# A StyleGAN-like convolution chain: one 7-tap convolution per sample in place of a blurred upsampling and a downsampling, and another order of the stages

## The chip, the cores and the metric

The kernel runs on one core of a Trainium2 chip. The metric is the device time of one execution in microseconds (us). The core has TensorE (PE, matmul; PEld is its weight load), VectorE (DVE), ScalarE (ACT), GpSimd (POOL) and SyncE (SP, here only DMA issue).

## The reference, cut to what matters

x has 128 samples of 32 channels by 512 positions. Four layers are applied; each is a conditioned chain of four small 1D convolutions (`_layer`), and a linear layer over the 512 positions (512 by 512) with a residual.

```
s = style @ mw.T + mb                     # 64 style numbers per sample -> 32
weight = SCALE * w * s[:, None, :, None]  # so every sample has its own 3-tap weights
weight = weight * rsqrt(sum(weight**2) + EPS)
'same':       conv(x, weight) + b
'upsample':   conv_transpose(x, weight, stride 2) + b, then blur with 2*[1,3,3,1]/8
'same':       conv(x, weight) + b
'downsample': blur with [1,3,3,1]/8, conv(stride 2) + b
y = x after the four convolutions
x = x + linear(y)   # layer 1: top-2 of 8 LoRA experts; layer 2: a LoRA chosen by sample group;
                    # layer 3: top-1 of 4 LoRA experts; layer 0: LoRAs folded into the weight
```

Upsampling, blurring, the third convolution, blurring and downsampling are linear, so they can be composed into fewer convolutions with longer kernels, apart from the few positions at each end.

## The kernel before, in words

Sixteen samples form a group: 4 row blocks of 32 channels fill the 128 partitions, times 4 columns. There are 8 groups and 4 layers, so 32 phases; phase n is one group in one layer, and two groups alternate, since phase n needs the result of phase n - 2. Eight phases make a step: two of layer 0, two of layer 1 and so on. The work of a loop turn n on PE is the convolutions of phase n and the linear layer of phase m = n - 1. Layers 0 and 2 are called plain below, layers 1 and 3 have an adapter.

Small tiles: the convolutions are matmuls of 32 by 32 (or 64 by 32, 32 by 64) weights, sixteen (or eight) of which stand side by side in the array. One step is one tap for all 16 samples. All convolution operands are fp32, and each matmul instruction has two records in the trace.

PE's order in a turn, written out by hand in the block at the end of `main_program`:

- `conv0(n)` (L1003): first convolution, 3 steps of 512 columns, 48 matmuls.
- `turn(m)` (L1078): 16 transposes of y3 into four PSUM banks; ACT copies them rounded (`y3t_hi`), DVE subtracts (`y3t_lo`).
- `conv2(n, 0)`, `conv2(n, 1)` (L1052): upsampling, blur and third convolution composed to per-sample kernels `wv`; 3 paired taps of 64 output columns, two single taps, and 16 one-column matmuls for the ends ("ghosts"), each.
- `adapter(m)` (L1095) in layers 1 and 3: 24 or 12 matmuls of 512 columns. It waits for all of `y3t_lo`.
- `base(m, b)` (L1137): 12 matmuls of 128 by 128 by 512 for each of four blocks of tokens b. In phases m % 8 = 1 and 4 `effective` (L1108) also makes the weights of the chosen LoRA, which DVE adds to a raw weight (`w_sum`, L957).
- `products(n + 1)` (L1027): products of the second and third convolutions' weights for the next phase, 5 steps (3 of 96 columns, 2 of 32). POOL then sums neighbours in three passes (`blurred`, L698).
- `down(n, 0)`, `down(n, 1)` (L1068): blur and downsampling, 3 taps, 48 matmuls of 64 by 32.

ACT and DVE evacuate each half of the banks (`evacuate_0`, `evacuate_2`, `evacuate_3`), POOL scales the input (`xs`, L716), adds the bias (L729) and makes the low halves of weights (`w_lo`, L723). Two sets of four PSUM banks exist, `bank_a` and `bank_b`, with fixed roles. Semaphores order everything; no scheduler reorders.

A first program (`setup_program`) computes styles, demodulation, end corrections (`bias_q`, L453) and weights, once; the main program starts when it is over.

## Time and profile before

| | |
|---|---|
| median of 3 runs | 1303.74 us (1299.21 to 1305.76) |
| profiled execution, its own time | 1306.01 us |
| its span | 1304.2 us |
| PE busy | 1233.0 us (95%) |
| DVE / ACT / POOL busy | 496.3 / 356.1 / 546.2 us |
| mean granted clock of TensorE | 0.987 |

PE records overlap, as matmuls are pipelined: the length of a stage is best read as the difference of two starts. The time of a group of small matmuls is the union of its records, not the mean of one times the count.

### The profile page before, as it was taken

The page shows a single profiled execution, that of the slowest core. Times are in us where ns is not written, and L with a number is a line of the kernel's source. Part 1 is how long each engine was busy: PE and PEld are TensorE (multiplying, and loading weights), DVE is VectorE, ACT ScalarE, POOL GpSimd, SP SyncE. Part 2 cuts the span into 40 slices and gives each one's busy share as a digit, 9 for nine tenths or more (in the row PEclk, how much of TensorE's full clock was granted, in tenths as well). Part 3 has the DMA queues.
Part 4 walks back from the last instruction along what each step waited for, and adds up shares of the span by engine and source line. Part 5 has one row for each costly group of instructions (what it writes and reads, how often), then busy time and mean ns, then how long its engine had stood idle before and what let it go on. Part 6 is the DMA issues. An engine that isn't in the chain of part 4 may idle for free.

```text
span 1304.2 us, 45847 instructions
## 1 busy us (share of the span) xinstructions
PE 1233.0 (95%) x21400; PEld 704.6 (54%) x21400; DVE 496.3 (38%) x975; ACT 356.1 (27%) x757; POOL 546.2 (42%) x417
## 2 busy tenths in 40 slices
PE   5847999999999999999999999999999999999997
PEld 5323556555555555565565555565565554665555
DVE  5612324344333333434333333434333434433343
ACT  2213313223322222313223222312323222312321
POOL 3156641444443442644323543644413544634400
PEclk9968999999999999999999999999999999999999
DMA  8232300002221200000301300000211200000101
GB/s 285 114 105 101 115 17 2 2 3 59 98 105 62 99 3 2 3 2 25 134 27 42 131 3 2 2 2 13 103 53 58 99 3 2 2 2 3 67 2 65
DMA packets 20828, 65.66 MB, mean 50 GB/s; under 512 B 4032, under 2 KB 4416, under 8 KB 16160
## 3 DMA queue, kind: packets, MB, share of 16 engines
q1 hardware_dynamic: 18960, 60.85, 12.8%
q8 instruction: 168, 2.75, 0.9%
q10 hardware_dynamic: 1680, 1.89, 0.5%
q14 instruction: 20, 0.16, 0.0%
HBM read 43.85 MB, written 18.87 MB: 48 GB/s over the span
## 4 chain that ended last, share of the span: by engine, by line
PE 87%; DVE 4%; POOL 1%; issue 1%; ACT 0%; DMA 0%; DVEq 0%; POOLq 0%
PE bank_b L1137 26%; PE bank_a L1068 13%; PE bank_a L1052 11%; PE bank_b L1052 11%; PE bank_b L1003 8%; PE bank_b L1095 5%; PE bank_a L1078 5%; PE bank_a L1027 3%; PE bank_b L1149 2%; PE bank_b L1118 1%; DVE w_sum L957 1%; PE bank_b L1130 1%; POOL xs L716 1%; POOL sum_v L698 1%; DVE z L939 1%
## 5 line engine op out<-in xcount | busy, mean ns | idle before, releaser
L698 POOL TENSOR_TENSOR sum_v<-raw_v 128x768 f32<-128x768 f32 x32 | 58.9, 1842 | 626.5 <-ACT raw_v L760 626.5
L1137 PE MATMUL bank_b<-w_hi,y3t_hi 128*128 128x512 f32 x512 | 210.0, 410 | 12.4 <-DVE w_sum L957 12.1
L1137 PE MATMUL bank_b<-w_hi,y3t_lo 128*128 128x512 f32 x512 | 203.0, 396 | 2.2 <-issue 2.2
L1137 PE MATMUL bank_b<-w_lo,y3t_hi 128*128 128x512 f32 x512 | 202.4, 395 | 0.1
L1068 PE MATMUL bank_a<-y,w_down 64*32 64x512 f32 x3072 | 173.6, 594 | 1.5 <-ACT wv L762 1.5
L1052 PE MATMUL bank_a<-y,wv 32*64 32x512 f32 (+2 forms) x3584 | 145.8, 480 | 2.3 <-issue 2.3
L1052 PE MATMUL bank_b<-y,wv 32*64 32x512 f32 (+2 forms) x3584 | 142.3, 480 | 1.8 <-ACT y L741 1.8
L895 DVE TENSOR_TENSOR x<-bank_b,x 128x512 f32<-128x512 f32 x96 | 66.4, 692 | 202.2 <-PE bank_b L1137 166.0
L753 ACT ACTIVATE y<-bank_a,cb,tab 128x512 f32<-128x512 f32 x64 | 49.7, 776 | 319.4 <-PE bank_a L1068 319.4
L1003 PE MATMUL bank_b<-xs,cw 32*32 32x512 f32 x3072 | 112.0, 615 | 15.3 <-POOL xs L716 15.3
L1137 PEld LDWEIGHTS bank_b<-w_hi,y3t_hi 128*128 128x128 f32 x512 | 96.8, 189 | 50.9 <-DVE w_sum L957 15.6
L1137 PEld LDWEIGHTS bank_b<-w_hi,y3t_lo 128*128 128x128 f32 x512 | 96.6, 189 | 25.9 <-issue 3.1
L1068 PEld LDWEIGHTS bank_a<-y,w_down 64*32 64x32 f32 x3072 | 55.3, 106 | 102.2 <-issue 102.2
L1137 PEld LDWEIGHTS bank_b<-w_lo,y3t_hi 128*128 128x128 f32 x512 | 97.0, 189 | 20.3 <-issue 0.6
L716 POOL TENSOR_TENSOR xs<-x,tab 128x512 f32<-128x512 f32 x96 | 97.3, 1043 | 8.9 <-DVE x L895 8.9
L1052 PEld LDWEIGHTS bank_a<-y,wv 32*32 32x32 f32 (+1 forms) x3584 | 45.0, 114 | 100.9 <-issue 100.4
L875 DVE TENSOR_SCALAR y<-bank_a,tab,cb 128x512 f32<-128x512 f32 x64 | 51.8, 810 | 121.4 <-PE bank_a L1068 121.4
L1003 PEld LDWEIGHTS bank_b<-xs,cw 32*32 32x32 f32 x3072 | 48.0, 104 | 76.5 <-issue 48.1
L854 DVE TENSOR_SCALAR y<-bank_b,tab 128x512 f32<-128x512 f32 x64 | 48.9, 807 | 100.8 <-PE bank_b L1003 100.8
L1052 PEld LDWEIGHTS bank_b<-y,wv 32*32 32x32 f32 (+1 forms) x3584 | 44.7, 114 | 76.4 <-issue 73.3
L881 DVE TENSOR_TENSOR y3t_lo<-bank_a,y3t_hi 128x512 fp32r<-128x512 f32 x128 | 79.5, 684 | 15.0 <-ACT y3t_hi L768 15.0
L861 DVE TENSOR_SCALAR y<-bank_a,tab 128x512 f32<-128x512 f32 x64 | 48.9, 806 | 90.4 <-PE bank_a L1052 90.4
(172 smaller groups left out, 1553.0 us busy)
## 6 DMA issues: line engine op xcount, KB each, us to landing
w_hi<-w_scratch SPq DMA_DIRECT2D x9, 1024.0 KB, 5.8
w_lo<-w_scratch SPq DMA_DIRECT2D x9, 1024.0 KB, 8.0
x_in<-in_x SPq DMA_DIRECT2D x32, 256.0 KB, 4.1
out_x<-out_tile SPq DMA_DIRECT2D x32, 256.0 KB, 2.4
w_raw<-w_scratch SPq DMA_DIRECT2D x3, 1024.0 KB, 9.8
w_scratch<-w_hi SPq DMA_DIRECT2D x3, 1024.0 KB, 3.9
w_scratch<-w_lo SPq DMA_DIRECT2D x3, 1024.0 KB, 6.9
w<-in_w SPq DMA_DIRECT2D x2, 1024.0 KB, 13.5
```

Of the source, the lines that this page charges most:

```text
L698: ins = g_.tensor_tensor(dst[:, :, at:at + count].rearrange("p r k o -> p r (k o)"), src[:, :, 0:count].rearrange("p r k o -> p r (k o)"), ...
L716: nc.gpsimd.tensor_tensor(xs[:, b, 1:LEN + 1], src[:, b], column(n, T_S, b).broadcast_to((P, LEN)), ALU.mult).then_inc(xs_ready, 1)
L753: a.activation(y3[:, r], bank_a[r][:], ACT.Identity, bias=keep["cb3"][:, layer(n):layer(n) + 1], scale=column(n, T_A + 3, r)).then_inc(y3_ ...
L875: v.tensor_scalar(y3[:, r], bank_a[r][:], column(n, T_A + 3, r), keep["cb3"][:, layer(n):layer(n) + 1], ALU.mult, ALU.add).then_inc(y3_dve, 1)
L881: v.tensor_tensor(y3t[1][:, k], bank_a[k][:], y3t[0][:, k].bitcast(F32), ALU.subtract).then_inc(y3t_ready, 1)
L895: v.tensor_tensor(result, lin_ps[b][:], x[g][:, b], ALU.add).then_inc(x_ready, 1)
L1003: ins = pe.matmul(banks[r][CH * c:CH * (c + 1)], weights[rows, l, block_], src[rows, (r + c) % ROWS, 1 + shift:1 + shift + LEN], start=(i ...
L1052: ins = pe.matmul(banks[r][to:to + CH * count, at:at + length], wv[rows, a, tap:tap + count].rearrange("p t o -> p (t o)"), y0[rows, a, st ...
L1068: ins = pe.matmul(bank_a[2 * u + h][CH * a:CH * (a + 1)], keep["down"][rows, layer(n), t], y2[u][rows, c, t:t + LEN], start=(t == 0), stop ...
L1078: ins = pe.transpose(bank_a[k][:, P * b:P * (b + 1)], y3[:, b, P * k:P * (k + 1)], ident[:])
L1095: ins = pe.matmul(ps[0:rows], a_l[ai][:, k, col:col + rows], y3t[yi][:, k], start=(k == 0 and i == 0), stop=(k == KB - 1 and i == 2))
L1137: ins = pe.matmul(lin_ps[b][:], y3t[yi][:, k, P * b:P * (b + 1)], w[use(m) % 2][wi][:, k], start=(k == 0 and i == 0), stop=(k == KB - 1 an ...
```

## The change

`conv2` and `down` are replaced by one convolution with seven taps at the sample's own resolution, `conv(n)`: 7 steps of 16 matmuls of 512 columns, and between them 6 steps of 16 one-column matmuls (`END_STEPS`) that correct the first and last positions. Its kernels `wv` come from two rounds of products on PE: `products_raw(n + 1)` (3 steps of 128, 96 and 128 columns; up times same) and `products_all(n)` (7 steps of 288, 224, 224, 192, 192, 96 and 96 columns; times a blurred down kernel from the setup). ACT and DVE evacuate them into `wr` and `wv`; POOL's `blurred` is gone. `evacuate_2` is gone too.

PE's turn is now `products_raw(n + 1)`, `products_all(n)`, `conv0(n)`, `turn(m)`, `linear_front(m)` (adapter, two of the four blocks, `effective`), `conv(n)`, `linear_back(m)`. The bank sets change roles each phase (`banks_x`, `banks_y`). In block 0 of `base` the matmuls with `y3t_hi` come before those with `y3t_lo`, each with its own wait. `turn` and `products_all` have new waits.

In the setup the end corrections take a second round of products through PE (`bias_3`), between the LoRA weights of layer 0 and the effective weights of layer 2, with DVE's down kernels before it; and the matmuls of layer 0's weights wait for `bias_2_ready` in place of `bias_copied`.

PE at the passage from a plain phase's linear layer to the next turn, where `wv` are the sample's kernels, `w_down` the down kernels and `w_hi`, `w_lo` the linear weights. Before:

```order
L1137 MATMUL bank_b<-w_hi,y3t_lo 128x512
L1068 MATMUL bank_a<-y_0,w_down 32x512 x24
L1068 MATMUL bank_a<-y_1,w_down 32x512 x24
L1003 MATMUL bank_b<-xs,cw 32x512 x48
L1078 MATMUL bank_a<-ident,y 128x128 x16
L1052 MATMUL bank_b<-y,wv 64x512 x8
L1052 MATMUL bank_b<-y,wv 32x1 x16
L1052 MATMUL bank_b<-y,wv 64x512 x16
L1052 MATMUL bank_b<-y,wv 32x512 x16
```

And now, to the same point:

```order
L1194 MATMUL bank_b<-w_hi,y3t_lo 128x512 x4
L1076 MATMUL bank_a<-w_up,w2s 32x128 x16
L1076 MATMUL bank_a<-w_up,w2s 32x96 x16
L1076 MATMUL bank_a<-w_up,w2s 32x128 x16
L1092 MATMUL bank_b<-w_down,wr 32x288 x16
L1092 MATMUL bank_b<-w_down,wr 32x224 x32
L1092 MATMUL bank_b<-w_down,wr 32x192 x32
L1092 MATMUL bank_b<-w_down,wr 32x96 x32
L1061 MATMUL bank_a<-xs,cw 32x512 x48
L1130 MATMUL bank_b<-ident,y 128x128 x16
L1189 MATMUL bank_a<-w_hi,y3t_hi 128x512
```

The products stand ahead of conv0, the down convolution is gone, and the linear layer follows the transposes at once; conv2 stood between them before.

PE in an adapter phase of layer 1, from the transposes on, now:

```order
L1061 MATMUL bank_b<-xs,cw 32x512 x48
L1130 MATMUL bank_a<-ident,y 128x128 x16
L1144 MATMUL bank_b<-y3t_hi,a_hi 128x512
L1144 MATMUL bank_b<-y3t_lo,a_hi 128x512
L1144 MATMUL bank_b<-y3t_hi,a_lo 128x512
```

The adapter's matmuls, which want `y3t_lo` whole, moved from behind conv2 to right behind the transposes.

PE in the setup, from the end corrections (`bias`) to the effective weights (`gmat`), before:

```order
L453 MATMUL w_ps<-bias_v,bias_q 128x64 x12
L463 MATMUL w_ps<-b,a 128x512 x8
L470 MATMUL mod_ps<-bs_raw,as_raw 128x512 x2
L470 MATMUL mod_v_ps<-bs_raw,as_raw 128x512
L470 MATMUL var_ps<-bs_raw,as_raw 128x512
L480 MATMUL w_ps<-b,gmat 128x512 x8
```

Now, where the rows for one of the four layers stand for all:

```order
L488 MATMUL w_ps<-bias,bias_w 32x32 x80
L498 MATMUL w_ps<-b,a 128x512 x8
L505 MATMUL mod_ps<-bs_raw,as_raw 128x512 x2
L505 MATMUL mod_x_ps<-bs_raw,as_raw 128x512
L505 MATMUL var_ps<-bs_raw,as_raw 128x512
L519 MATMUL w_ps<-bias,bias_dn 32x32 x8
L519 MATMUL w_ps<-bias,w_dn 32x32 x24
L519 MATMUL w_ps<-bias,bias_dn 32x32 x4
L519 MATMUL w_ps<-bias,w_dn 32x32 x8
```

In all 176 small matmuls came in ahead of the effective weights.

The diff, cut to its core:

```diff
-RAW, TAPS_V, GHOSTS = 2 * TAPS - 1, 2 * TAPS + 2, 2
-PAIRS_V = ((3, 0), (1, 1), (5, -1))
-PAD = 2
+RAW = 2 * TAPS + 1
+RAW_STEPS = ((0, 0, 0, TAPS + 1), (1, 2, 1, TAPS), (2, 3, 1, TAPS + 1))
+REACH = TAPS
+ALL, MID = 2 * REACH + 7, REACH + 3
+PAD = REACH
+ALL_STEPS = ((3, 2, 9, 9), (1, 5, 2, 7), (5, 1, 0, 7), (2, 5, 20, 6), (4, 2, 18, 6), (6, 10, 26, 3), (0, 0, 29, 3))
+END_STEPS = ((0, LEN - 1, LEN - 2), (1, LEN - 2, LEN - 1), (2, LEN - 1, LEN - 1), (10, 0, 0), (11, 1, 0), (12, 0, 1))
...
+                    f = slice(GF * i, GF * (i + 1))
+                    ins = v.tensor_tensor(
+                        table[:, i, 2 * h:2 * h + 2, T_B3:T_B3 + BIASES], sums[:, :, :, f],
+                        scale_3[:, 2 * h:2 * h + 2, f].unsqueeze(2).broadcast_to((P, 2, BIASES, GF)), ALU.mult)
+                ins.then_inc(bias_3_read, 1)
...
-            pe.wait_ge(bias_copied, 2)
+            pe.wait_ge(bias_2_ready, 1)
...
                 pe.matmul(w2_ps[p], as2[:, p * P:(p + 1) * P], bs2[:], start=True, stop=True).then_inc(w2_done, 1)
+            for l in range(LAYERS):
+                for kind, terms in enumerate(bias_3):
+                    for i, (tap, which, of) in enumerate(terms):
+                        for r in range(ROWS):
+                            rows = slice(CH * r, CH * (r + 1))
+                            weights = bias_dn[rows, l, which] if tap == "all" else w_dn[rows, l, 1 + tap]
+                            last = pe.matmul(bias_out(l, kind, rows), weights, bias_2[rows, l, of],
+                                             start=(i == 0), stop=(i == len(terms) - 1), skip_group_check=True)
+            last.then_inc(bias_3_done, 1)
...
-    z_ps, logit_ps = bank_b[0], bank_b[1]
-    zt_ps = logit_ps
-    lin_ps = [bank_b[2], bank_b[3], bank_b[0], bank_b[1]]
+    def banks_x(n):
+        return (bank_a, bank_b)[n % 2]
+    def banks_y(n):
+        return (bank_b, bank_a)[n % 2]
+    def raw_bank(n):
+        return banks_x(n - 1) if n else banks_y(0)
...
-            def blurred(n):
...
-                chain_ = ((raw_v, sum_v[0], 1), (sum_v[0], sum_v[1], 1), (sum_v[1], wv, 0))
-                                           src[:, :, 1:count + 1].rearrange("p r k o -> p r (k o)"), ALU.add)
-                    ins.then_inc(v_sums if i < 2 else wv_ready, 1)
             pool.wait_ge(halos_zero, 1)
             scaled_weights(0)
-            blurred(0)
+            scaled_weights(1)
...
+                if n + 2 < PHASES:
+                    scaled_weights(n + 2)
...
                 m, convolve, linear = n - 1, n < PHASES, n > 0
+                if n + 1 < PHASES:
+                    products_raw(n + 1)
                 if convolve:
+                    products_all(n)
                     evacuate_0(n)
                 if linear:
                     turned(m)
-                if convolve:
-                    evacuate_2(n, 0)
-                    evacuate_2(n, 1)
-                if linear:
                     adapter(m)
                     exponentials(m)
-                if n + 1 < PHASES:
-                    products(n + 1)
+                if convolve:
+                    evacuate_3(n)
                 if linear:
                     adapter_turned(m)
                 if n in MADE_IN:
                     weights_hi(MADE_IN[n])
-                if convolve:
-                    evacuate_3(n)
...
-                    evacuate_2(n, 1)
                 if plain:
                     residual(m, 0)
+                    effective(m)
                     residual(m, 1)
-                    effective(m, 0)
+                elif linear:
+                    gated(m)
+                if convolve:
+                    evacuate_3(n)
+                    ends(n)
+                if plain:
                     residual(m, 2)
                     residual(m, 3)
-                    effective(m, 1)
                 elif linear:
-                    gated(m)
                     adapter_turned(m)
                     for b in range(ROWS):
                         residual(m, b)
-                if convolve:
-                    evacuate_3(n)
...
+            def products_raw(n):
+                pe.wait_ge(w2s_ready, n + 1)
+                if n >= 2:
+                    pe.wait_ge(y3_act, evacuated(n - 2))
+                    pe.wait_ge(y3_dve, evacuated(n - 2))
+                for i, (tap, at, first, count) in enumerate(RAW_STEPS):
...
+                            ins = pe.matmul(raw_bank(n)[r][CH * c:CH * (c + 1), CH * at:CH * (at + count)],
+                                            w2s[rows, (r + c) % ROWS, CH * tap:CH * (tap + 1)],
+                                            keep["up"][rows, layer(n), first:first + count].rearrange("p k o -> p (k o)"),
+                                            start=(i == 0), stop=True, skip_group_check=True)
+                ins.then_inc(raw_done, 1)
+            def products_all(n):
+                pe.wait_ge(wr_act, evacuated(n))
+                pe.wait_ge(wr_dve, evacuated(n))
                 if n >= 2:
                     pe.wait_ge(x_ready, tiles(n - 2, ROWS))
-                    if (n - 2) % STEP in EFF:
...
+                            ins = pe.matmul(banks_y(n)[r][CH * b:CH * (b + 1), CH * at:CH * (at + count)],
+                                            wr[n % 2][rows, (b - r) % ROWS, block_],
+                                            keep["down"][rows, layer(n), first:first + count]
+                                            .rearrange("p k o -> p (k o)"),
+                                            start=(i == 0), stop=True, skip_group_check=True)
+                ins.then_inc(all_done, 1)
+            def conv(n):
+                pe.wait_ge(y0_act, evacuated(n))
+                pe.wait_ge(y0_dve, evacuated(n))
+                pe.wait_ge(wv_act, evacuated(n))
+                pe.wait_ge(wv_dve, evacuated(n))
+                if n:
                     pe.wait_ge(y3t_ready, tiles(n - 1, KB))
-                banks = (bank_b, bank_a)[u]
-                steps = [(tap, 2, 0, PAD + shift, LEN, 0) for tap, shift in PAIRS_V]
...
+                    if (n - 1) % STEP in EFF:
+                        pe.wait_ge(w_sum_ready, summed(n - 1) + KB)
+                steps = [(MID + shift, PAD + shift, LEN, 0) for shift in range(-REACH, REACH + 1)]
+                for i, (block_, col, to) in enumerate(END_STEPS):
+                    steps.insert(2 * i + 1, (block_, PAD + col, 1, to))
...
+                            rows, a = slice(CH * r, CH * (r + 1)), (r + d) % ROWS
+                            ins = pe.matmul(banks_y(n)[r][CH * a:CH * (a + 1), to:to + length],
+                                            wv[rows, (r - a) % ROWS, block_], y0[rows, a, start:start + length],
+                                            start=(i == 0), stop=(i == len(steps) - 1), skip_group_check=True)
+                ins.then_inc(cv_done, 1)
...
                 pe.wait_ge(y3t_ready, tiles(m, KB))
-                if convolve:
-                    pe.wait_ge(y2_ends, 2 * (m + 1) + 1)
-                else:
-                    pe.wait_ge(x_ready, tiles(m - 1, ROWS))
+                left(m)
...
+                    if b == 0:
+                        pe.wait_ge(y3t_hi, tiles(m, k + 1))
+                    for wi in range(2):
+                        pe.matmul(lin_bank(m, b)[:], y3t[0][:, k, tokens], w[use(m) % 2][wi][:, k],
+                                  start=(k == 0 and wi == 0), stop=False)
+                for k in range(KB):
+                    if b == 0:
+                        pe.wait_ge(y3t_ready, tiles(m, k + 1))
+                    ins = pe.matmul(lin_bank(m, b)[:], y3t[1][:, k, tokens], w[use(m) % 2][0][:, k],
+                                    start=False, stop=(k == KB - 1 and l in (0, 2)))
...
-            def weights(m, convolve):
-                if convolve:
-                    pe.wait_ge(y2_ends, 2 * (m + 1) + 1)
+            def left(m):
+                if m + 1 < PHASES:
+                    pe.wait_ge(y0_act, evacuated(m + 1))
+                    pe.wait_ge(y0_dve, evacuated(m + 1))
...
+            def linear_front(m):
+                adapter(m)
+                weights(m)
+                base(m, 0)
+                to_tokens(m)
+                effective(m)
+                base(m, 1)
...
             for n in range(PHASES + 1):
-                m, convolve, linear = n - 1, n < PHASES, n > 0
-                adapts = linear and layer(m) in (1, 3)
-                if convolve:
+                m = n - 1
+                if n + 1 < PHASES:
+                    products_raw(n + 1)
+                if n < PHASES:
+                    products_all(n)
                     conv0(n)
-                if linear:
+                if m >= 0:
                     turn(m)
-                if convolve:
-                    conv2(n, 0)
-                    conv2(n, 1)
-                if adapts:
-                    adapter(m, convolve)
-                if linear:
-                    pe.wait_ge(y3t_ready, tiles(m, KB))
-                    weights(m, convolve)
-                    base(m, 0)
-                    if adapts:
-                        to_tokens(m)
-                        base(m, 1)
-                        effective(m, 0)
-                if n + 1 < PHASES:
-                    products(n + 1)
-                if adapts:
+                    linear_front(m)
+                if n < PHASES:
+                    conv(n)
+                if m >= 0:
                     linear_back(m)
-                elif linear:
-                    base(m, 1)
-                    effective(m, 0)
-                    if m % STEP in EFF:
-                        pe.wait_ge(w_sum_ready, summed(m) + 2)
-                    base(m, 2)
-                    base(m, 3)
-                    effective(m, 1)
-                if convolve:
-                    down(n, 0)
-                    down(n, 1)
```

## Rows read from the trace of the kernel before

**Rows 1.** Page, busy time of the engines, share of the span, instructions.

```profile
PE 1233.0 (95%) x21400; PEld 704.6 (54%) x21400; DVE 496.3 (38%) x975; ACT 356.1 (27%) x757; POOL 546.2 (42%) x417
```

**Rows 2.** PE's waits from 180 us on: us in total, times, longest us.

```profile
PE bank_b L1137 <- DVE w_sum L957: 12.1, 8, 1.5
...
PE bank_b L1095 <- DVE y3t_lo L881: 1.9, 1, 1.9
```

**Rows 3.** Timeline of PE, one turn: start us, length us, what, count.

```profile
612.74 5.39 PE L1068 MATMUL bank_a<-y,w_down 64*32 64x512 f32 x96
618.05 3.40 PE L1003 MATMUL bank_b<-xs,cw 32*32 32x512 f32 x96
621.39 1.97 PE L1078 MATMUL bank_a<-ident,y 128*128 128x128 f32 x16
623.29 4.45 PE L1052 MATMUL bank_b<-y,wv 32*64 32x512 f32 x112
...
632.04 0.50 PE L1137 MATMUL bank_b<-w_hi,y3t_hi 128*128 128x512 f32 x1
...
635.04 1.85 PE L1027 MATMUL bank_a<-w2s,w_up 32*32 32x96 f32 x160
636.82 0.51 PE L1137 MATMUL bank_b<-w_hi,y3t_hi 128*128 128x512 f32 x1
637.16 0.39 PE L1137 MATMUL bank_b<-w_lo,y3t_hi 128*128 128x512 f32 x1
637.39 0.39 PE L1137 MATMUL bank_b<-w_hi,y3t_lo 128*128 128x512 f32 x1
```

**Rows 4.** Groups by shape, PE: busy us, mean ns of one, idle.

```profile
L1052 PE MATMUL bank_a<-y,wv 32*32 32x1 f32 x1024 | 12.1, 175 | 1.3 <-issue 1.3
```

**Rows 5.** Timeline of ACT and DVE behind the same conv0.

```profile
621.50 1.53 DVE L854 TENSOR_SCALAR y<-bank_b,tab 128x512 f32<-128x512 f32 x2 [2.44 <-PE bank_b L1003]
622.84 2.06 ACT L768 ACTIVATE y3t_hi<-bank_a 128x512 fp32r<-128x512 f32 x4
...
623.47 2.48 DVE L881 TENSOR_TENSOR y3t_lo<-bank_a,y3t_hi 128x512 fp32r<-128x512 f32 x4 [0.44 <-ACT y3t_hi L768]
```

**Rows 6.** Windows: busy us and count of PE, PEld, DVE, ACT, POOL; granted clock.

```profile
170.00:173.40 3.40, 1.77 (x138) 1.43 (x138) 0.69 (x1) 0.00 (x0) 0.00 (x0) 1.00 0.02 5
173.50:176.90 3.40, 3.40 (x39) 2.72 (x30) 0.00 (x0) 1.36 (x8) 1.67 (x1) 0.50 0.02 5
```

**Rows 7.** Timeline of PE at that place.

```profile
172.93 0.94 PE L1027 MATMUL bank_a<-w2s,w_up 32*32 32x96 f32 x67 [1.63 <-issue]
173.81 0.80 PE L1137 MATMUL bank_b<-w_hi,y3t_hi 128*128 128x512 f32 x1
...
176.94 0.39 PE L1137 MATMUL bank_b<-w_lo,y3t_hi 128*128 128x512 f32 x1
```

**Rows 8.** Timeline of the setup and of the main program's first turns.

```profile
6.13 3.64 PE L429 MATMUL mod_ps<-cond,mod_w 64*32 64x64 f32 x128 [6.13 <-DMA mod_w<-in_mod_w]
...
34.88 9.82 PE L463 MATMUL w_ps<-b,a 128*128 128x512 f32 x16 [1.05 <-ACT bias L224]
...
39.62 1.29 DVE L383 COPY tab<-mod 128x128 f32<-128x128 f32 x1
...
69.70 2.50 PE L1027 MATMUL bank_a<-w2s,w_up 32*32 32x96 f32 x160 [7.44 <-POOL w2s L685]
...
83.96 5.16 PE L1003 MATMUL bank_b<-xs,cw 32*32 32x512 f32 x96 [11.76 <-POOL xs L716]
...
150.18 4.99 POOL L723 TENSOR_TENSOR w_lo<-w_raw,w_hi 128x512 fp32r<-128x512 f32 x4
...
191.79 3.41 PE L1003 MATMUL bank_b<-xs,cw 32*32 32x512 f32 x96
```

**Rows 9.** Page, DMA issues: count, KB each, us to landing.

```profile
w_raw<-w_scratch SPq DMA_DIRECT2D x3, 1024.0 KB, 9.8
```

More of the change, by code:

```diff
@@ L342, in _ @@
-            dve.wait_ge(blocks, 2 * TAPS)
-            for g in range(ROWS):
-                rows = slice(CH * g, CH * (g + 1))
-                v.tensor_copy(keep["down"][rows], w_dn[rows, :, TAPS * (g % 2):TAPS * (g % 2 + 1)])
+            for kind, tap in ((2, taps[0]), (3, taps[2])):
+                v.tensor_scalar(bias_w[:, :, kind], tap, -0.25, None, ALU.mult)
+            then(v.tensor_scalar(bias_w[:, :, 0], taps[1], -0.25, None, ALU.mult))
+            for kind, tap in ((1, taps[0]), (4, taps[2])):
+                ins = v.scalar_tensor_tensor(out=bias_w[:, :, kind], in0=tap, scalar=-2.0, in1=bias_w[:, :, 0],
+                                             op0=ALU.mult, op1=ALU.add)
@@ L944, in gated, with effective @@
                 ins.then_inc(z_ready, 1)
-            def effective(m, half):
+            def effective(m):
                 if m % STEP not in EFF:
@@ L1058, in down @@
[L1058 to L1071 removed]
+                            rows, b = slice(CH * r, CH * (r + 1)), (r + d) % ROWS
```

495 lines of the change are left out of this document (238 added, 257 removed).

## The prediction

> **What bounds the kernel now.** I read the page's busy shares first: PE is busy 95% of the span, every other engine under half of it [rows 1]. Then PE's waits: behind 180 us they come to some 20 us, the largest being 12.1 us for `w_sum` in eight pieces [rows 2]. So in the steady part the time is PE's instruction stream, and the change is worth what it takes from that stream less the waits that its new order makes. The timeline of one turn gives the length of each stage as the difference of two starts [rows 3]: products 1.78 us (635.04 to 636.82), down 5.31, conv0 3.34, transposes 1.90, both halves of conv2 8.75, together 19.18 us of small tiles beside the transposes; a 128 by 128 by 512 matmul follows its forerunner by 0.23 us (637.16 to 637.39), so that four blocks cost 11.2 us.
>
> **Small tiles, part by part.** A step is 16 tiles side by side. Products are 5 steps with 352 columns in all in 1.78 us, conv0 3 steps with 1536 columns in 3.34 us [rows 3]. A line through both: 0.235 us a step and 0.00172 us a column. By it
> - `products_raw`: 3 steps, 352 columns: 0.71 + 0.60 = 1.31 us.
> - `products_all`: 7 steps, 1312 columns: 1.65 + 2.25 = 3.90 us.
> - conv0: as before, 3.34 us.
> - `conv`: 7 steps of 512 columns, 7.79 us, and 6 end steps of one column at 0.24 us, 1.42 us.
> That is 17.76 us against 19.18: 1.42 us less a turn. The end steps are the least sure: 1024 records of one column were busy for 12.1 us [rows 4], which is 0.38 us for the 32 records of a step. I take 0.24, since the two products steps of 32 columns come close to it; the ends are 0 (all hidden under the columns' stream, 1.42 us less) and 0.38 (0.84 us more). `products_all` runs along widths that the trace lacks, between 96 and 512 columns; from its bare columns (2.25 us) to seven conv0 steps scaled by width plus 0.38 each (4.9 us) I take the line. The first large matmul behind small ones costs 0.34 us in place of 0.23 (636.82 to 637.16) [rows 3]; two stretches in place of three save one such passage, 0.1 us.
>
> The Trainium skill has a rule against this part, in TensorEngine Tiling (Array Packing), Instruction Overhead: each matmul carries about 60 cycles, and one column lasts as long as 60. As an estimate that is 25 ns a record at 2.4 GHz, 0.8 us an end step, and the sum would be about 105 us longer. The trace disagrees: 12.1 us over 1024 records is 12 ns each.
>
> **What goes away outside PE.** POOL's three sums for each phase go, with ACT's and DVE's evacuations of conv2. None of these was waited for in the steady part [rows 2], so I give them nothing. The new evacuations (`wr`, `wv`) lie under `products_all` (3.9 us) and conv0 (3.3 us).
>
> **The waits.** Per turn, from 191.79 us on, which is the conv0 of turn 3, there are 29 turns and the last linear layer: 15 with an adapter, 14 plain, 7 of the plain ones with `effective`.
> - `effective`: before, PE waited 1.5 us for `w_sum` since the banks were wanted by the next block [rows 2]. Now block 1 (2.8 us) lies between, and the four DVE additions (about 0.6 us each) end as it ends. -1.5 us x 7 = -10.5.
> - Adapter: it needs all of `y3t_lo`. DVE ends it at 625.95 (623.47 + 2.48), since ACT and DVE first evacuate y0 from 621.50 on [rows 5]; the transposes end at 623.29 [rows 3]. conv2 covered this before. The order of ACT and DVE at this place is unchanged, and PE has nothing between. So PE now waits 2.7 us, x 15 = +40.5. Behind the waiting matmul stands all of the linear layer, and behind that conv. This is the cost of the new order.
> - Plain: block 0 takes each `y3t_hi` as it comes; the first is there at about 623.45, the last at 624.90 [rows 5], and PE uses two matmuls (0.47 us) for each 0.5 us of ACT. 0.2 us x 14 = +2.8.
> - `products_all(n)` waits for the last residual of phase n - 2. That comes about 0.9 us behind its matmul, and `products_raw` (1.3 us) covers it. Conv0 wants POOL's `xs` about 2 us into the turn, and gets 5.2. If `products_raw` did not cover it, 0.5 us a turn would be lost.
>
> **The clock.** The granted clock fell to 1.2 GHz at 173.5 us, behind an idle of 1.63 us inside the products [rows 6, 7]. The eight waits of 1.5 us never did this. The new wait of 2.7 us lies beyond both. In the slow stretch 13.4 matmuls would have fitted where 7 stood (173.81 to 176.94) [rows 7]: 1.5 us lost each time. The one wait of 1.9 us, at the end [rows 2], left the clock up, so not each will do it. I take 10 of 15: +15 us (0 to 23).
>
> **The start.** Setup: the matmuls of `w0` started at 34.88. They now wait for a DVE chain that holds the table operations, of which the copy at 39.62 ended at 40.9 [rows 8], plus about 1.6 us of new products: 42.5, so +7.6. `bias_3` adds 176 small matmuls, four side by side; 64 such took 3.64 us [rows 8], 0.057 each: +10.0. Their sparse work may bring the clock down for the effective weights: +1.5. Together +19 (12 to 24).
> Main program: from the first product (69.70) to 191.79 went 122.1 us, with 11.76 us of waiting for `xs` behind POOL's sums [rows 8]. Now turn 0 is two raw products at half clock (2 x 1.31 x 1.4, the ratio of 2.50 to 1.78), `products_all` 5.5, conv0 5.2, y0 1.8, conv 10.7, y3 1.8: 28.7 us. Turn 1 is 31.2 (1.31 + 3.90 + 3.34 + 1.90 + 0.2 + 11.2 + 9.21 and passages) and 1.5 of slow clock. Turn 2 has `effective` (1.1), slow clock again (1.5), and a wait that is new: POOL's `w_lo` (4.99 us) ends 8 us into the turn, and only then may SP store it and reload `w_raw`, 9.8 us to landing and about 2 us in the queue [rows 8, 9]; the additions end at 22.3 us where conv could start at 17.2: 5 us. 38.8 us. In all 100.2, so -22 (-30 to -12).
> The end: the wait of 1.1 us for y3 becomes one for the last residual, 0.
>
> **Sum.** -1.42 x 29 = -41.2; passages -2.9; `effective` -10.5; plain +2.8; adapters +40.5; clock +15; setup +19; start -22: +0.7 us. On the profiled execution's 1306.0 that is 1306.7; this stands 2.3 us over the median, so I predict 1304.5 us. About 0.5% (6.5 us) is what a measurement tells from no change.
>
> **Rivals.**
> 1. Faster, 1281 us: the same order of stages, but the end steps ride under the columns' stream (half of the 1.42 us, x 31 = -22), or the clock stays up (-15), or both in part. For it: in one of two cases with a long idle the clock stayed at 2.4 GHz [rows 2]. Against it: conv0's steps take 1.07 to 1.11 us where their columns ask 0.88, so the tiles have no free time that one-column steps could use.
> 2. Slower, 1330 us: one mechanism, the end step as a break in the tiles' overlap. Each costs 0.38 us as in rows 4 and no less, +0.84 us x 31 = +26. It decides from 0.28 us an end step on (+7 us). For it: the row itself. Against it: in the row the steps stand between two tile shapes.
> 3. By the skill's rule above the end steps would be dearer yet. As rows have it: two latencies of 0.175 us for both records [rows 4], 0.70 us a step, +0.46 x 6 x 31 = +86, 1390 us. Little speaks for it.
> 4. PE's order isn't what binds: the longer stream of records (832 small ones a turn in place of 576) is fetched late. It would show as idles put down to issue. 1.3 us at the longest so far in the steady part; at 1 us a turn +30, 1335 us, slower too.
>
> **Chances.** No change by the sum: 0.36, its own range 1292 to 1317. Rival 1: 0.32. Rival 2: 0.25. Rival 3: 0.02. Rival 4: 0.05. Of the first, a seventh falls under 1297 and as much over 1310. So faster 0.37, same 0.26, slower 0.37. The range reaches well into rivals 1 and 2: 1275 to 1338.
>
> **What would show it.** Right: PE idle ahead of the adapter (L1144) for `y3t_lo`, about 2.7 us x 15; the wait for `w_sum` gone but for one long piece; products_raw and products_all together 5.2 us; conv 9.2 us; the granted clock at 0.5 in some ten short stretches, each behind a wait of the adapter; main program starting some 19 us later. Wrong: conv at 8 us or at 10 us and more, `products_all` off the line by over 1 us, a clock that stays up, or idles put down to issue.

## The result, and the profile after

The changed kernel takes 1467.47 us (median of 4 runs, 1459.19 to 1470.63) against 1304.72 us: ratio 1.125, 95% interval 1.119 to 1.131. It is 163 us slower where 1304.5 us was forecast, far outside the range of 1275 to 1338. The span of the profiled execution went from 1304.2 to 1468.8 us.

The page: engines; then the DMA queue of instructions (packets, MB, share); then the chain of work that ended last, by engine.

```profile
PE 1271.8 (87%) x30080; PEld 833.0 (57%) x30080; DVE 459.0 (31%) x988; ACT 270.2 (18%) x500; POOL 343.5 (23%) x316
...
q8 instruction: 236, 3.87, 1.1%
...
PE 77%; issue 8%; ACT 4%; DVE 3%; DMA 1%; POOL 1%; SPq 0%; DVEq 0%
```

PE is busy 39 us more than before [rows 1] in a span 165 us longer: its share fell from 95 to 87%. So most of the loss is idle time, which "issue" leads. PE's waits from the first product on (us in total, times, longest us):

```profile
PE bank_b L1092 <- issue: 32.3, 21, 4.6
PE bank_a L1092 <- issue: 28.6, 20, 3.5
PE bank_b L1144 <- DVE y3t_lo L929: 21.5, 8, 2.7
PE bank_a L1144 <- DVE y3t_lo L929: 20.4, 8, 2.7
PE bank_b L1061 <- issue: 11.9, 10, 3.5
PE bank_b L1117 <- issue: 10.2, 14, 1.2
PE bank_a L1117 <- issue: 10.0, 14, 1.5
...
PE bank_a L1061 <- issue: 6.3, 8, 1.3
...
PE bank_b L1117 <- DVE w_sum L1005: 0.8, 1, 0.8
```

`w_sum` is gone as a wait (12.1 us in rows 2), the adapters wait 2.7 us each, and 99 us of idle stand inside `products_all` (L1092), conv0 (L1061) and `conv` (L1117) with nothing to wait for. One `products_all` shows their pattern (start, length, what, count, idle before):

```profile
981.24 1.74 PE L1092 MATMUL bank_a<-w_down,wr 32*32 32x288 f32 x69
983.81 2.21 PE L1092 MATMUL bank_a<-w_down,wr 32*32 32x224 f32 x128 [0.84 <-issue]
987.56 0.43 PE L1092 MATMUL bank_a<-w_down,wr 32*32 32x96 f32 x24 [1.53 <-issue]
```

From stall to stall run exactly 128 matmul records. With their weight loads these are 256, and the page has 236 instruction packets for 60,160 records of PE and PEld: one packet for 255 records. The DMA rows of 980 to 992 us, in slices of 0.3 us, show those packets and nothing else:

```profile
GB/s 0 0 0 55 0 0 0 0 0 0 0 0 0 0 0 0 55 0 0 0 0 0 0 0 0 0 0 0 0 55 0 0 0 0 0 0 0 0 0 0
DMA packets 3, 0.05 MB, mean 4 GB/s; under 512 B 0, under 2 KB 0, under 8 KB 0
```

Packets of 16 KB start at about 981.0, 984.9 and 988.8 us, 3.9 us apart. Matmuls resume at 983.81 and 987.56, 2.6 to 2.8 us behind a packet's start; the next packet starts about 1.2 us behind the resumption. PE thus runs through one packet while the next comes. Over the whole run 16 of the 235 intervals between packets are under 3.45 us, the shortest 3.2. 128 products need 2.2 us.

In `conv` the stall is shorter, since 128 of its records (two steps and two end steps) last longer:

```profile
909.24 3.96 PE L1117 MATMUL bank_a<-y,wv 32*32 32x512 f32 x166
913.40 2.82 PE L1117 MATMUL bank_a<-y,wv 32*32 32x1 f32 x128 [0.20 <-issue]
917.14 2.80 PE L1117 MATMUL bank_a<-y,wv 32*32 32x1 f32 x122 [0.93 <-issue]
```

Again 3.74 us for 128 records. Not each stall shows as idle: the conv from 863.89 to 874.51 us has no idle in its row and yet takes 10.62 us, where 9.2 was due.

The long stalls are another thing. In this one 219 records of products had run since 671.01:

```profile
672.26 2.50 PE L1092 MATMUL bank_b<-w_down,wr 32*32 32x288 f32 x120
679.37 2.50 PE L1092 MATMUL bank_b<-w_down,wr 32*32 32x192 f32 x99 [4.61 <-issue]
```

The DMA rows of 671 to 683 us, again in slices of 0.3 us:

```profile
GB/s 0 0 0 273 0 137 164 355 410 382 437 437 437 410 410 437 437 437 410 464 410 382 137 27 0 27 27 0 0 0 0 0 0 55 0 0 0 0 0 0
...
q8 instruction: 2, 0.03, 1.0%
```

SP loads `w_hi` and `w_lo` (2 MB) from 672 to 678 us, and only two instruction packets come in those 12 us, where the quiet window had three. All six stalls over 2 us in the steady part (2.1 to 4.6 us) have such data packets beside them.

The clock, windows of a wait ahead of an adapter, the adapter behind it, and what follows (columns as in rows 6, then the DMA share and GB/s):

```profile
590.00:599.60 9.60, 6.75 (x151) 3.87 (x151) 5.01 (x8) 4.32 (x8) 5.37 (x5) 1.00 0.01 3
599.70:606.90 7.20, 7.15 (x24) 4.41 (x25) 0.00 (x0) 0.00 (x0) 0.00 (x0) 0.76 0.00 0
607.00:615.00 8.00, 8.00 (x65) 5.65 (x64) 3.03 (x17) 1.29 (x3) 0.00 (x0) 1.00 0.00 0
```

Behind 2.7 us of idle the clock is at 1.2 GHz for part of the adapter, which takes 7.2 us in place of 5.7. 12 of 16 adapters did this.

Setup, PE and the first product (rows 8 have those of before):

```profile
41.45 8.61 PE L498 MATMUL w_ps<-b,a 128*128 128x512 f32 x16 [10.57 <-DVE bias L369]
...
53.62 0.33 PE L519 MATMUL w_ps<-bias,bias_dn 32*32 32x32 f32 x16
...
63.45 9.57 PE L533 MATMUL w_ps<-b,gmat 128*128 128x512 f32 x16
72.85 7.03 PE L533 MATMUL w_ps<-a,gmat 128*128 128x512 f32 x16
86.47 2.06 PE L1076 MATMUL bank_b<-w_up,w2s 32*32 32x128 f32 x96 [6.58 <-POOL w2s L752]
```

`bias_3` (L519) stalls too, by the waits of the whole run:

```profile
PE w_ps L519 <- issue: 5.4, 2, 3.6
```

### The profile page after: what moved, and what is told of

Read it like the earlier page. It is cut to its first block, busy times and chain, and to the rows that moved or that the text cites. A ratio compares the mean times of both kernels' runs of the same rounds, so it can differ in the third digit from the quotient of the medians.

```text
span 1468.8 us, 62798 instructions
## 1 busy us (share of the span) xinstructions
PE 1271.8 (87%) x30080; PEld 833.0 (57%) x30080; DVE 459.0 (31%) x988; ACT 270.2 (18%) x500; POOL 343.5 (23%) x316
## 4 chain that ended last, share of the span: by engine, by line
PE 77%; issue 8%; ACT 4%; DVE 3%; DMA 1%; POOL 1%; SPq 0%; DVEq 0%
PE bank_b L1117 11%; PE bank_a L1117 11%; PE bank_b L1189 8%; PE bank_a L1189 8%; PE bank_b L1061 4%; PE bank_a L1092 4%; PE bank_b L1092 4%; PE bank_a L1061 4%; PE bank_b L1194 4%; PE bank_a L1194 4%; PE bank_a L1144 3%; PE bank_b L1144 3%; ACT y L794 3%; DVE y3t_lo L929 3%; PE bank_b L1076 2%
## 5 line engine op out<-in xcount | busy, mean ns | idle before, releaser
L1117 PE MATMUL bank_b<-y,wv 32*32 32x1 f32 (+1 forms) x6656 | 170.0, 402 | 13.3 <-issue 10.2
L1117 PE MATMUL bank_a<-y,wv 32*32 32x1 f32 (+1 forms) x6656 | 169.2, 402 | 10.6 <-issue 10.0
L1117 PEld LDWEIGHTS bank_b<-y,wv 32*32 32x32 f32 x6656 | 87.0, 103 | 88.2 <-issue 72.9
L1117 PEld LDWEIGHTS bank_a<-y,wv 32*32 32x32 f32 x6656 | 86.9, 103 | 84.1 <-issue 70.4
L1189 PE MATMUL bank_a<-w_hi,y3t_hi 128*128 128x512 f32 x256 | 104.0, 406 | 1.9 <-ACT y3t_hi L817 1.9
L1189 PE MATMUL bank_b<-w_hi,y3t_hi 128*128 128x512 f32 x256 | 104.1, 407 | 1.5 <-ACT y3t_hi L817 1.3
L1189 PE MATMUL bank_b<-w_lo,y3t_hi 128*128 128x512 f32 x256 | 101.0, 395 | 0.0
L1189 PE MATMUL bank_a<-w_lo,y3t_hi 128*128 128x512 f32 x256 | 101.0, 394 | 0.0
L1092 PE MATMUL bank_b<-w_down,wr 32*32 32x224 f32 (+3 forms) x3584 | 71.5, 340 | 32.6 <-issue 32.3
L1092 PE MATMUL bank_a<-w_down,wr 32*32 32x192 f32 (+3 forms) x3584 | 69.2, 332 | 29.4 <-issue 28.6
L1092 PEld LDWEIGHTS bank_b<-w_down,wr 32*32 32x32 f32 x3584 | 53.2, 105 | 48.1 <-issue 40.6
L1061 PE MATMUL bank_b<-xs,cw 32*32 32x512 f32 x1536 | 69.2, 635 | 11.9 <-issue 11.9
L785 POOL TENSOR_TENSOR x<-x,ob 128x512 f32<-128x512 f32 x64 | 79.2, 1269 | 0.0
L1092 PEld LDWEIGHTS bank_a<-w_down,wr 32*32 32x32 f32 x3584 | 52.0, 104 | 44.2 <-issue 36.6
L1061 PE MATMUL bank_a<-xs,cw 32*32 32x512 f32 x1536 | 69.4, 640 | 6.5 <-issue 6.3
L1194 PE MATMUL bank_b<-w_hi,y3t_lo 128*128 128x512 f32 x256 | 69.8, 394 | 0.0
```

The lines of the kernel that those rows point to most:

```text
L785: nc.gpsimd.tensor_tensor(x[g][:, b], src[:, b], keep["ob"][:, l], ALU.add).then_inc(xb_ready, 1)
L1061: ins = pe.matmul(banks_x(n)[r][CH * b:CH * (b + 1)], keep["cw"][rows, 0, layer(n), t], xs[rows, b, t:t + LEN], start=(t == 0), stop=(t == ...
L1092: ins = pe.matmul(banks_y(n)[r][CH * b:CH * (b + 1), CH * at:CH * (at + count)], wr[n % 2][rows, (b - r) % ROWS, block_], keep["down"][row ...
L1117: ins = pe.matmul(banks_y(n)[r][CH * a:CH * (a + 1), to:to + length], wv[rows, (r - a) % ROWS, block_], y0[rows, a, start:start + length], ...
L1189: pe.matmul(lin_bank(m, b)[:], y3t[0][:, k, tokens], w[use(m) % 2][wi][:, k], start=(k == 0 and wi == 0), stop=False)
L1194: ins = pe.matmul(lin_bank(m, b)[:], y3t[1][:, k, tokens], w[use(m) % 2][0][:, k], start=False, stop=(k == KB - 1 and l in (0, 2)))
```

## The experiments

Theory F: PE's instructions come in packets of 256 records, one each 3.5 us or so at best; where PE uses them faster it stalls. Theory P, the rival: small steps are dearer than the line of the prediction says. Lengths of stages below are sums over the run of differences of starts. `ends_x3_1`, `no_ends_1` and `before_ghosts` are one execution each; they move the time by 113 us and more, while the executions of one kernel above lie within 12 us.

**More end steps, none.** `ends_x3_1`:

```diff
-                    steps.insert(2 * i + 1, (block_, PAD + col, 1, to))
+                    for _ in range(3):
+                        steps.insert(4 * i + 1, (block_, PAD + col, 1, to))
```

> The changed kernel with each of the six end steps issued three times (the surplus ones add to the same columns, so the ends of the output are others); 384 one-column records more a turn. Theory F: conv has 800 records, 6.25 packets; at 3.5 us a packet less some 1.5 packets that are there at its start, 17 to 21 us, and 1700 us in all (1640 to 1770), with idles for issue of over 5 us in each conv. Price by the line of the prediction (0.24 us a step): conv 12.1 us, 1467 + 0.9 x 31 = 1495 us. Theory P (0.5 us a step): conv 16.8 us, 1467 + 5.6 x 31 = 1640 us, without more idle than now.

Measured 1836.5 us, over both. `conv` took 712.7 us, 22.3 us each for 800 records: 27.8 ns a record, 3.56 us for 128 on average. The page has 332 packets, 96 more for 24,576 records more of PE and PEld:

```profile
q8 instruction: 332, 5.44, 1.2%
```

And PE's waits:

```profile
PE bank_b L1118 <- issue: 68.7, 82, 2.0
PE bank_a L1118 <- issue: 67.9, 78, 3.4
```

P dies by its own number (1640 us, no more idle). The granted clock speaks against a price of PE's own as well: it was at 1.2 GHz for most of 23 of the convs, which took 22.2 us on average, and the six that ran wholly at 2.4 GHz took 21.9. F's 1700 us was too low. I had taken 1.5 packets as being in hand at the start of a stretch, where 6.25 packets at 3.56 us account for all 22.3 us and leave next to none; and `base` was 19.5 us longer at the lower clock.

`no_ends_1`:

```diff
-                for i, (block_, col, to) in enumerate(END_STEPS):
+                for i, (block_, col, to) in enumerate(()):
```

> The changed kernel with the six end steps of conv left out (the end corrections are not computed; 192 of 832 small matmul records a turn go). Theory F (fetch): PE's instructions come in packets of 16 KB, 256 records of matmul and weight load each, and in a dense stretch one packet comes each 3.5 us or later; so 128 small matmul records never take less than about 3.5 us for long. conv is then 224 records and 7.8 us, 34.8 ns a record, slower than the fetch, and its idles put down to issue vanish (20.2 us now); conv falls from 11.2 to 7.8-8.0 us, and products_all and conv0 gain a little since a packet more is there when they start: 1340 us (1325 to 1360). Theory P (price: an end step in conv costs about 0.5 us, not 0.24, and the idles are the trace's own): conv 7.8 us too, products_all and conv0 unchanged: 1362 us.

Measured 1354.2 us, between F's 1340 and P's 1362, so the time alone decides nothing. `conv` is 245.5 us, 7.7 each, as 224 records ask, and has no idle for issue among its leading waits; `products_all` and conv0 kept theirs (61.5 and 16.3 us), so what F hoped for there did not come. The six end steps thus cost 0.60 us each in `conv`, and the twelve more of `ends_x3_1` 0.92 each: no fixed price of a step gives both.

**The kernel before, made dense.** `before_ghosts`, in `conv2`:

```diff
-                steps[1:1] = [(TAPS_V, 1, 0, PAD, 1, 0), (TAPS_V + 1, 1, 1, PAD + LEN - 1, 1, LEN - 1)]
+                steps[1:1] = [(TAPS_V, 1, 0, PAD, 1, 0), (TAPS_V + 1, 1, 1, PAD + LEN - 1, 1, LEN - 1)] * 4
```

> The kernel before the change with each of conv2's two one-column steps issued four times: 192 one-column records more a turn (as many as the changed kernel's end steps have), the rest as before (the surplus adds to the end columns). Theory F: both halves of conv2 have 480 records, 3.75 packets at 3.57 us = 13.4 us less up to a packet in hand, where they took 8.75: +3 to +4.6 us a turn, 1303 + 118 = 1421 us (1390 to 1450), with idles put down to issue. By the line of the prediction alone, 0.24 us for 32 records: +1.4 x 32 = +46, 1349 us, without such idles. If the fetch stalls belonged to the changed kernel's code (its order, its banks) and not to the density of records, 1349 us too.

Measured 1478.5 us: 192 more one-column records a turn cost 177 us, where their own price is 46. `conv2` grew from 288.0 to 446.6 us in all. PE's waits now have in the old kernel what the new one had:

```profile
PE bank_b L1052 <- issue: 29.5, 17, 5.0
PE bank_a L1052 <- issue: 21.7, 19, 1.9
PE bank_a L1027 <- issue: 11.7, 7, 2.2
```

So the order, the banks and the code of the change are not needed for the stalls; the density is enough. The expected 1421 us was too low, although it counted too many records: `conv2` has 416 of them here and 224 in the kernel before, where I had 480 and 288. At 27.8 ns a record 416 would take 11.6 us. The stage took 12.9 us in the 21 turns without data packets beside it and 16.0 us in the other 11. Each half now issues 128 one-column records in a row, a whole packet in about 1.2 us; whether that makes the difference to 11.6 was not tested.

**Same instructions, other places.** `split_1`:

```diff
                 for i, (block_, start, length, to) in enumerate(steps):
+                    if i == 6 and m >= 0:
+                        base(m, middle(m))      # 2 in phases with effective, else 1
```

It lacks block 1 of the very last linear layer (2.8 us).

> The changed kernel with one block of the linear layer (12 matmuls of 512 columns, 2.8 us) moved into the middle of conv, behind its sixth step: same instructions, other places. Block 1, or block 2 in the phases with effective. Theory F: while the block runs a packet comes in, so conv without the block falls from 11.2 to about 9.9 us: -1.3 x 31 = -40 us, 1427 us (1410 to 1445). Theory P: nothing but two more passages of 0.1 us, 1473 us. The idle of 2.7 us ahead of the adapter stays in both.

Measured 1424.6 us, ratio 1.093 (1.091 to 1.095): -43 us, or -40 without the missing block, as F said. `conv` without the block is 41 us shorter, and its idle for issue fell from 20.2 to 5.7 us, with all its instructions still there.

`turn_first_1`, PE's order (ACT and DVE likewise), with the waits for free banks moved along:

```diff
-                    products_all(n)
-                    conv0(n)
                 if m >= 0:
                     turn(m)
-                    linear_front(m)
+                if n < PHASES:
+                    conv0(n)
+                    products_all(n)
+                if m >= 0:
+                    linear_front(m)
```

> The changed kernel with PE's order products_raw, turn, conv0, products_all, linear_front in place of products_raw, products_all, conv0, turn, linear_front (ACT and DVE in the same order). The evacuation of y3t then lies under conv0 and products_all. Both theories: the 2.7 us ahead of the adapter's matmuls go (-42 us), and with them the stretches of 1.2 GHz in the adapter (-1.5 us x 12 = -18). Theory F: the transposes (1.9 us, 16 records) stand between the small stages, so that about one packet wait of 1 us a turn goes, -30: 1377 us (1360 to 1395). Theory P: 1407 us. What could speak against both: conv0 is earlier by 2 us and may wait for xs, +0.5 us a turn.

Measured 1339.5 us, ratio 1.028 (1.025 to 1.032): -128 us by order alone. The transposes' stage fell from 108.5 to 63.4 us, the adapters from 86.0 to 70.4 (clock 0.983), the three small stages ahead of `conv` by 73, more than twice F's 30; why so much more was not tested. conv0 never waited for `xs`. One adapter wait is left of sixteen:

```profile
PE bank_a L1093 <- issue: 21.3, 17, 4.4
PE bank_b L1093 <- issue: 12.7, 14, 1.4
PE bank_a L1118 <- issue: 11.3, 14, 1.8
PE bank_b L1118 <- issue: 8.3, 14, 0.9
...
PE bank_a L1143 <- DVE y3t_lo L930: 1.9, 1, 1.9
```

**Both, and woven.** `both` joins the two edits: the diffs of `split_1` and `turn_first_1` together.

> turn_first and split together: transposes ahead of conv0 and products_all, and one block of the linear layer in the middle of conv (block 1 of an adapter phase or a plain one, block 2 in phases with effective). Theory F: both gains add up, as they hit other places: 1339.5 - 40 = 1299 us (1290 to 1312), so about level with the kernel before. If the packets that come in under the block were of no use to conv (theory P), 1343 us.

Measured 1325.7 us, ratio 1.018 (1.016 to 1.021): 14 us gained of the 40. `conv` with all its stalls lost 29 us, but the block that moved had been the cover of other places: the packets stall `products_all` as before (36 us), and `base` is 8 us longer.

`woven` cuts finer:

```diff
+            LUMPS_ALL = (2, 5)                                # halves of block 0, or of the adapter
+            LUMPS_CONV = ((2, 0, 4), (6, 4, 8), (10, 8, 12))  # step, matmuls of the middle block
```

> turn_first with PE's large matmuls woven into the small ones so that no 128 small records stand in a row: two halves of block 0 (or of the adapter's matmuls) behind the second and fifth step of products_all, and block 2 (block 1 in adapter phases) in three pieces of four matmuls behind steps 2, 6 and 10 of conv. Same instructions, other places. Theory F: each run of 128 small records now has at least 1 us of large matmuls in it and takes 3.5 us or more by itself, so the stalls of conv (57.9 - ... by stages: 357.9 us where 32 clean ones of 9.2 are 294) and of products_all (173 where 121 are due) go nearly: -105 us; ten more passages between large and small tiles a turn at 0.1 us cost +31: 1265 us (1250 to 1290). Without the fetch as the cause only the passages count: 1370 us.

Measured 1333.7 us, missed by 69. Most of the stalls did go: under 12 us of idle for issue are left. The price of a cut was over one and a half times the 0.2 us (two passages) that I took. PE's timeline in one conv:

```profile
719.28 0.51 PE L1213 MATMUL bank_a<-w_hi,y3t_hi 128*128 128x512 f32 x1
...
720.41 2.85 PE L1130 MATMUL bank_b<-y,wv 32*32 32x512 f32 x128
723.19 0.50 PE L1213 MATMUL bank_a<-w_hi,y3t_hi 128*128 128x512 f32 x1
...
724.31 2.85 PE L1130 MATMUL bank_b<-y,wv 32*32 32x512 f32 x128
```

Four large matmuls take 1.13 us (719.28 to 720.41) where 0.93 are due, and the end step ahead of them 0.57 in place of 0.44 us: 0.33 us a cut, 51 us for five cuts in 31 turns, where I had 31. Another 18.6 us went to `w_sum`, which had lost its cover. These are 39 of the 69 us; the rest is not accounted for. This run also gives the clean price of `conv`: 128 records in 2.78 us with no stall, the longer end step at the cut included, where the prediction's line says 2.70.

**The weight loads.** `after_late`:

```diff
+                    sp.wait_ge(tr_done, tiles(n - 1, KB))
                     load_weights(...)                 # at all three places
```

> The changed kernel; only SP issues the nine loads of linear weights (2 x 1 MB each, w_hi and w_lo from the scratch) behind the transposes of the turn in place of at its start, by one more wait. The stalls for issue of over 2 us in the changed kernel all stand in products_all or conv0 while data packets run, behind these loads. Theory F with data traffic as a second cause (a fetch is late when the data queue's packets are in its way): the turns with such a load lose 2 to 3.5 us less, 9 x 3 = -27 us: 1440 us (1430 to 1452). If the two only coincide: 1467 us. If the loads now hold up conv's packets instead: 1467 us too, with long stalls in conv.

Measured 1440.7 us, ratio 1.106 (1.103 to 1.109): -27 us as expected, in part by luck. Between the two profiled executions (spans 1468.8 and 1437.0 us) the small tiles lost 22 us, nearly all in `products_all` (15.7) and conv0 (5.8). Another 8.9 us came from the adapters, of which 6 of 16 were slowed by the clock in place of 12, though they wait as long as before. The longest stalls of `products_all` are gone from the waits (1.7 us for 4.6):

```profile
PE bank_b L1095 <- issue: 24.0, 21, 1.7
PE bank_a L1095 <- issue: 22.8, 20, 1.7
```

`both_late`, on `both`:

```diff
+                    sp.wait_ge(all_done, n + 1)
                     load_weights(...)
```

> both (transposes first, one block in the middle of conv) with the nine weight loads issued behind products_all, so that they run under the adapter and block 0, where PE uses few instructions. By the same reasoning: 1325.7 - 12 to -20 = 1310 us (1302 to 1318); if data traffic does not matter, 1326 us.

Measured 1332.3 us, 6.5 us worse. The idle of `products_all` fell from 35.8 to 26.7 us, that of `conv` rose from 9.5 to 22.6, as if the loads were now in conv's way.

**One cut in each stretch.** `all_late`, on `both_late`:

```diff
                 for i, (block_, at, first, count) in enumerate(ALL_STEPS):
+                    if i == 4 and m >= 0:
+                        first_large(m)          # the adapter, or block 0
```

> both_late, and products_all cut once: block 0 (the adapter's matmuls in adapter phases) behind its fourth step; in the phases with effective seven of block 2's matmuls stand ahead of conv and five in its middle. A cut between large and small tiles cost 0.35 us in woven (four matmuls of a block 1.13 us where 0.93 are due, and the small step before it 0.13 us longer), so +11 us; the stalls in products_all, 35.8 us in both, go to about 8: -27. In all 1310 - 16 = 1294 us (1284 to 1306), if the price of a cut is right; if a whole block in products_all helps no more than the three small pieces of woven did, 1315 us.

Measured 1301.2 us (10 runs), ratio 0.9995 (0.998 to 1.001), level with the kernel before. Stalls in `products_all` are gone from PE's leading waits; `conv` keeps 18 us.

```profile
PE bank_b L1128 <- issue: 10.0, 11, 1.8
PE bank_a L1128 <- issue: 8.1, 11, 1.6
```

`all_back`:

```diff
-                    sp.wait_ge(all_done, n + 1)
+                    sp.wait_ge(cv_done, n + 1)
```

> all_late with the nine weight loads issued behind conv (when cv_done comes) in place of behind products_all. They take 8 us and then run under the last linear blocks (5.7 us) and products_raw, the transposes and conv0, whose 128 records take 3.6 us or more by themselves, and no longer under the first half of conv, where the stalls of 1.2 to 1.8 us of all_late with data packets beside them stand (seven of them, about 10 us). 1301 - 8 = 1293 us (1287 to 1300). If the loads do not matter any more: 1301 us. If they now stall products_raw and conv0 instead: 1305 us.

Measured 1307.6 us, ratio 1.002 (0.999 to 1.005): a miss. In the profiled execution, the fastest of the ten at 1297.2 us, `conv`'s stalls fell from 18.1 to 8.8 us, but SP's new wait stands ahead of the output stores in its queue, and PE's waits for `out_tile` rose from 1.2 to 8.2 us:

```profile
PE bank_b L1139 <- DVE out_tile L949: 8.2, 4, 3.1
PE bank_b L1128 <- issue: 6.4, 10, 1.2
```

The two about cancel there (spans 1295.4 and 1295.2 us). What makes the median of the ten 10 us longer than this execution, no trace shows.

**The setup.** `all_setup` moves PE's matmuls of layer 2's weights and of two of layer 0's blocks ahead of the wait for `bias_2`:

```diff
+    W0_ORDER = (2, 3, 0, 1)
-            for p in range(KB):
+            for p in W0_ORDER:
+                if p == 0:
+                    pe.wait_ge(bias_2_ready, 1)
```

> all_back, and in the setup PE fills its wait of 10.6 us for bias_2 (DVE's chain): the four matmuls of layer 2's weights (L505, 3.6 us) and the two column blocks of layer 0's weights whose banks the end corrections do not use (4.3 us of L498) come ahead of that wait. Nothing behind it depends on their order but PE's own stream, so -7.9 us, if the inputs of both are loaded by then (in the changed kernel's trace bs2 and as2 landed long before 31 us is not shown; if they are late, 0): 1285 us (1279 to 1294). Against the kernel before, 1303: faster by 1.3%.

Measured 1305.2 us, a miss (ratio to `all_back` about 1). The wait of 10.6 us became one of 6.3 for the next DVE chain, and the first product came only 0.9 us sooner:

```profile
53.33 0.44 PE L518 MATMUL w_ps<-bias,bias_dn 32*32 32x32 f32 x16 [6.34 <-DVE bias_dn L404]
```

`late_setup`, on `all_late` with that order:

```diff
+            for y in (w_dn, *sum_dn): ...       # down to bias_dn, then_inc(down_ready, 1)
             dve.wait_ge(var_done, 1)
```

> all_late with two edits in the setup: PE's reordering of all_setup (layer 2's four matmuls and two blocks of layer 0's weights ahead of the wait for bias_2), and DVE's chain of the down kernels (L372 to L403, up to bias_dn), which needs only cw, moved ahead of DVE's wait for var_done, where DVE is idle for 7.1 us. In all_setup PE's gain of 8 us came back as a wait of 6.3 us for that chain (bias_dn). Now the chain is over by about 30 us in the program, bias_2 comes 1 us later, and bias_3 follows w0 at once: the first product at 78 to 80 us in place of 86, so 1301.2 - 7 = 1294 us (1288 to 1299). If something else holds the setup's end (a DMA, POOL's weights, the scratch stores), 1301 us.

Measured 1297.7 us (9 runs), ratio to the kernel before 0.994 (0.991 to 0.997); 3.6 us better than `all_late`, half of what was expected. The setup gave what was forecast, as the first product came at 80.1 us in place of 86.1; why the medians show only part of it is open. The wait is 0.7 us now, and the first small matmuls of `bias_3` stand at 49.57 us; its 352 matmul records stall as they did before:

```profile
49.57 0.33 PE L519 MATMUL w_ps<-bias,bias_dn 32*32 32x32 f32 x16 [0.69 <-ACT w_add L242]
...
53.63 0.22 PE L519 MATMUL w_ps<-bias,bias_dn 32*32 32x32 f32 x2 [2.28 <-issue]
```

It is the one version that beats both kernels, by 0.6%.

## Why the prediction was wrong, point by point

The difference of the spans, 164.6 us, by stages:

| term | predicted | measured |
|---|---|---|
| small tiles, start and passages | -66 | +99.8 (652.4 to 752.2) |
| waits of the adapters | +40.5 | +45.9 (transposes' stage 62.6 to 108.5) |
| clock | +15 | +18.1 (adapter 67.9 to 86.0) |
| `effective` | -10.5 | -14.2 (21.6 to 7.4) |
| block 0 in plain phases | +2.8 | -3.5 (all of `base`) |
| setup | +19 | +16.8 (first product 69.70 to 86.47) |
| the rest | 0 | +1.7 |

- **The step that failed** is the first: the line of 0.235 us a step and 0.00172 us a column was used as if nothing else could bind, and rival 4, the instruction stream that comes late, got 1 us a turn and a chance of 0.05. Its mechanism is what happened. In the 29 turns from 197 us on, the three small stages took 346.3 us where the line gives 246.6, `conv` 325.0 where it gives 267.1: 5.4 us a turn, not 1. That is 158 us of the gap of 166 in the table's first row; the rest lies in the start, where the first two turns took 18.8 and 16.8 us for these three stages, partly at 1.2 GHz. The first three turns took 110.5 us (86.47 to 196.96) where 100.2 were forecast, though of the 5 us of waiting for `w_sum` in turn 2 only 0.8 came.
- **The line itself held.** Clean steps cost what it says (2.78 for 2.70 us at a cut; `conv` without end steps 7.7 for 7.8). Rivals 2 and 3, the dear end step, and rival 1, the free one, are all wrong: an end step by itself costs about 0.24 us, as taken, but where the fetch binds its 32 records take a quarter of a packet, 0.89 us.
- **What the rows had shown.** [Rows 7] hold the idle of 1.63 us for issue behind 93 of 160 products. It ends 2.4 us behind the start of an instruction packet (170.56 us), as the stalls of the changed kernel do. The products before ran at 11 ns a record, but only 160 records at a time, and conv2 ran 224 records in 8.75 us [rows 3], 39 ns each; `ends_x3_1` finds 27.8 ns for what the fetch gives. The new `conv` asks for 22 ns a record over 416 records, `products_all` for 17 over 224. I counted 832 records for 576 and divided neither by time.
- **Adapter waits, clock, `effective`, setup**: right in kind and within 6 us each. In the setup the matmuls of `w0` start 6.6 us later (7.6 forecast), `bias_3` takes 9.8 us (10.0 forecast), and the first half of the effective weights behind it takes 2.4 us more, at a granted clock of 0.65 (1.5 forecast); the rest is 2.0 us less. The 10.0 is luck: 5.4 of the 9.8 us are idle for issue, and the 176 matmuls themselves take 4.4, less than half of the price.
- **What stays open**: why a packet needs 3.5 us when its own transfer lasts about 1, and how a data transfer delays it; `after_late` shows that moving nine loads took 22 us out of the small tiles, not by what way.

The Trainium skill, Runtime: NRT & Kernel Launch, Instruction fetch mechanics, has instructions come in blocks of 16 KiB, 256 each, the next while the current one runs. This trace agrees (255 records a packet). It also says that dispatch is slower than the filling, so that fetch is hidden. The measurement disagrees: 3.56 us a block on average in `ends_x3_1`, where 128 matmul records of `conv` want 2.7 us.

## What to carry to other kernels

Divide the instructions of each dense stretch by its time before trusting prices: here a stretch of small tiles whose 128 fp32 matmul records want less than 3.6 us was bound by the fetch of instructions. A large block in the middle of such a stretch costs 0.33 us and gives a stall back; here one cut in each stretch (`all_late`, 1301.2 us) did better than five a turn (`woven`, 1333.7 us). Read what a new order takes away from its neighbours too: each cover that moved here (block 1 for `w_sum`, conv2 for `y3t_lo`, SP's queue for the stores) came back as a wait.

## What the runs showed of the hardware that was not expected

- A packet of PE's instructions is 256 records of matmul and weight load, and under full demand one comes each 3.56 us on average (`ends_x3_1`; inside its convs 3.3 to 4.2 us apart); next to nothing is held beyond the packet being run and the next one. This does not follow TensorE's granted clock (22.2 us a conv with most of it at 1.2 GHz, 21.9 wholly at 2.4).
- Where 2 MB of data loads start with a dense stretch, PE stalled for 2.1 to 4.6 us at one place; issued behind the transposes, nine such loads cost the small tiles 22 us less.
- Part of a fetch stall does not show as idle but as a stage longer than its steps: 10.62 us with no idle, where 9.2 was due.
